# The six groups of 16 rows of each q and k stack, interleaved with a step of six rows

## The chip, the cores and the metric

The kernel runs on one core of a Trainium2 chip. The metric is the device time of one launch in microseconds (us), the median of three runs. One profiled execution gives the trace; its times are counted from the start of its span.

## What is computed

One transformer-like layer on 16 sequences: a cross-attention over a band of 129 positions, and a mixture of 16 experts with a shared expert. All is float32. The part that the change touches is the product of q and k:

```python
qkv = x @ w_in.T + b_in                      # x: layernorm of (16, 128, 512), transposed
q, k, v = jnp.split(qkv, 3, axis=-1)         # 8 heads of 16 channels, 512 positions
scores = jnp.einsum('bqhd,bkhd->bhqk', q, k) / jnp.sqrt(d)
band = jnp.abs(idx[:, None] - idx[None, :]) <= 64
attn = softmax(where(band, scores, neg))
o = einsum('bhqk,bkhd->bqhd', attn, v) ; out = w_ct(relu(o @ w_out.T) * encodings)
x = x + out ; x = x + ffn(layernorm(x))      # top-2 of 16 experts, and a shared one
```

## The kernel before, in words

Every engine has its own instruction list, written out by hand; semaphores join them. The attention part runs in steps U from -25 to 160, eight steps (`UNITS`) to a sequence, and a sequence passes through some 65 steps, so that several are under way together. In each step every engine does its share in a fixed order. The order on an engine is that of the code: an instruction that waits holds up all that stands behind it on that engine. This holds for SyncE (SP), which issues the DMAs of this part, too.

To get float32 accuracy out of bf16 matmuls, q is split into three bf16 parts (`qparts`, 128 partitions by 3 parts by 512 positions; the partition is channel times 8 plus head), and k likewise. A score is then one matmul with a contraction over 96 rows (`STACK` = 6 x 16): six pairs of parts, 16 channels each. The stacks `qstack` and `kstack` hold these rows for eight heads, [96 rows, 8 heads, 512 positions] in bf16, in a ring of four. A stack is filled by six DMAs from SBUF to SBUF. One DMA (line 305 for q, 310 for k) takes one part from all 128 partitions, 1 KB each, and writes it to 16 rows of the stack, 8 KB each: 128 KB. Group g lies in rows 16g to 16g+15. The parts become ready one after another, so the DMAs are issued in five steps: q with groups 0; 1 and 3; 2 and 4; 5 (steps -11, -10, -9, -8 of the sequence), k with groups 0; 2, 5 and 1; 4 and 3 (steps -7, -6, -5).

Line 555 (`scores`) multiplies the stacks over 96 rows, VectorE takes row maxima of the result (line 1100), GpSimd splits the maxima into three bf16 parts (lines 429 to 435), TensorE turns them, VectorE copies them to `mrows` (1108), and line 331 sends them, 24 KB, to rows 96 to 98 of `qstack` (step 9). Line 571 (`shifted_scores`, step 11) waits for this landing (`max_in`, line 567) and multiplies over 99 rows, so that the maximum is subtracted; ScalarE takes the exponential (899), GpSimd cuts the band (441, 443), and TensorE multiplies with v (585).

On SP's list, the three DMAs of line 327 (reciprocals of the sequence three before, 8 KB each, ready when GpSimd has run lines 416 to 422) stand ahead of the last q DMA (group 5 of another sequence, line 305), and this stands right ahead of line 331. Behind it come k's group 0 (310), the load of the encodings (352) and the other five DMAs of k. Line 315 fetches the denominators from every 32nd partition (`D:P:32`), so the kernel has one DMA already that steps over partitions. Before the first sequence, SP loads 6.8 MB of inputs (lines 294 to 301).

After the attention come the shared expert (385 to 520 us, with the loads of the routed experts' weights) and the routed experts, bound by TensorE.

Of the kernel before, what the change touches and what calls it, by code (L numbers as in the profile page):

```python
# [34 lines left out]
HEADS, D = 8, 16  # L35
# [11 lines left out]
STACK = 6 * D  # L47
UNITS = 2 * QB
RING = 4
# [53 lines left out]
def xattn_moe_kernel(nc, x, ctx_in, const_f, const_b, w_small, w_gu, w_d, sw_gu, sw_d, out):  # L103
    es = ExitStack()
    with es:
# [28 lines left out]
        def over(shape, dt=F32):  # L134
            cols = 1
            for s in shape:
                cols *= s
            words = cols if dt is F32 else (cols + 1) // 2
            ap = wgu[:, used[0]:used[0] + words]
            used[0] += words  # L140
            assert used[0] <= EXPERTS * 4 * 512
            if dt is not F32:
                ap = ap.bitcast(dt)
            if len(shape) == 1:
                return ap
            names = " ".join("abc"[:len(shape)])
            return ap.rearrange(f"p ({names}) -> p {names}", **{"abc"[i]: s for i, s in enumerate(shape)})

        qstack = [over([HEADS, T], BF16) for _ in range(RING)]
        kstack = [over([HEADS, T], BF16) for _ in range(RING)]  # L150
# [142 lines left out]
        def _(sp):  # L293
# [8 lines left out]

            def send_q(n, groups):
                for g in groups:
                    sp.dma_start(qstack[n % RING][D * g:D * g + D, :, :],
                                 qparts[:, Q_PARTS[g], :]).then_inc(q_in[n % RING], 16)

            def send_k(n, groups):
                for g in groups:
                    sp.dma_start(kstack[n % RING][D * g:D * g + D, :, :],  # L310
                                 kparts[:, K_PARTS[g], :]).then_inc(k_in[n % RING], 16)

            def denominators(n, g):
# [6 lines left out]
            def step(U):  # L320
# [11 lines left out]
                if (n := at(U, -11)) is not None:  # L332
                    after(sp, s2_ready, 2 * UNITS * (n - RING + 1))
                    sp.wait_ge(q_p1, n + 1)
                    send_q(n, (0,))
# [3 lines left out]
                if (n := at(U, -10)) is not None:  # L339
                    send_q(n, (1, 3))  # L340
                if (n := at(U, -9)) is not None:
                    sp.wait_ge(q_p2, n + 1)
                    send_q(n, (2, 4))
# [3 lines left out]
                if (n := at(U, -7)) is not None:  # L347
                    sp.wait_ge(k_p1, n + 1)
                    send_k(n, (0,))
# [3 lines left out]
                if (n := at(U, -6)) is not None:  # L353
                    send_k(n, (2, 5))
                    sp.wait_ge(k_p2, n + 1)
                    send_k(n, (1,))
# [1093 lines left out]
```

## Time and profile before

| | |
|---|---|
| runs | 783.01, 787.33, 787.78 us; median 787.33 us |
| profiled execution | 781.99 us, its span 780.3 us |
| TensorE busy | 670.5 us of the span (86%) |
| VectorE, ScalarE, GpSimd busy | 401.3, 355.2, 438.6 us |
| DMA, mean | 122 GB/s, 95.17 MB |
| TensorE's granted clock | 0.944 of full speed |

Busy shares are means over stages with different limits. The chain of work that ended last is read back from the last instruction, at each step to what released it. A DMA in the chain stands with the time from its issue to its landing. DMA share is the mean busy share of the core's 16 DMA engines; it can come out a little over 1.

### The profile page before, as it was taken

How to read it: one execution, taken by the hardware profiler on the slowest of the kernel's cores; microseconds unless marked ns; L12 is line 12 of the kernel's file. 1: busy time of each engine (PE TensorE's matmuls, PEld its weight loads, DVE VectorE, ACT ScalarE, POOL GpSimd, SP SyncE). 2: the span in 40 equal slices, each digit the busy share in tenths (PEclk: the TensorE clock that was granted, in tenths of full speed). 3: DMA queues.
4: the chain of work that ended last, by engine and by line, in shares of the span. 5: the costliest groups of instructions: out<-in, count | busy, mean ns of one | idle time of the engine just before them, and what ended most of it. 6: DMA issues, size and time to landing. Idle time of an engine off the chain costs nothing.

```text
span 780.3 us, 14074 instructions
## 1 busy us (share of the span) xinstructions
PE 670.5 (86%) x4136; PEld 329.9 (42%) x4136; DVE 401.3 (51%) x1439; ACT 355.2 (46%) x670; POOL 438.6 (56%) x640
## 2 busy tenths in 40 slices
PE   3179789988889988888778979989999999999992
PEld 1035445555555555553333535533333333333330
DVE  3297788888888888862332276332222322222210
ACT  2126666666666666555212111223444444444441
POOL 1377777777777777756310000023776766766763
PEclk9578999999999999998978998999999999999997
DMA  9968656666666666411496752523456465564530
GB/s 326 167 95 94 98 83 103 105 109 105 112 113 112 113 112 112 80 31 32 162 366 204 263 181 67 174 97 66 104 120 142 103 155 108 112 145 78 86 46 0
DMA packets 64472, 95.17 MB, mean 122 GB/s; under 512 B 18064, under 2 KB 42768, under 8 KB 62224
## 3 DMA queue, kind: packets, MB, share of 16 engines
q1 hardware_dynamic: 50048, 66.75, 39.3%
q0 software_dynamic: 9600, 18.89, 12.9%
q10 hardware_dynamic: 4752, 8.65, 3.4%
q8 instruction: 35, 0.57, 0.4%
q14 instruction: 37, 0.30, 0.2%
HBM read 50.99 MB, written 19.14 MB: 90 GB/s over the span
## 4 chain that ended last, share of the span: by engine, by line
PE 58%; POOL 12%; DMA 9%; issue 7%; DVE 6%; SPq 5%; ACT 3%; ACTq 0%; DVEq 0%; POOLq 0%
PE bank L731 18%; PE bank L761 9%; PE bank L718 7%; DMA wgu<-wgu 7%; PE bank L749 4%; POOL wgu L443 4%; POOL wgu L441 3%; PE bank L711 3%; SPq L327 3%; PE bank L571 3%; PE bank L555 3%; PE bank L742 2%; PE bank L585 2%; PE bank L597 2%; DVE bank L1100 2%
## 5 line engine op out<-in xcount | busy, mean ns | idle before, releaser
L1100 DVE CUSTOM_DVE_ANT_0 bank<-bank,cb 128x192 f32<-128x192 f32 (+1 forms) x512 | 187.1, 415 | 53.7 <-PE bank L555 52.4
L899 ACT ACTIVATE wgu<-bank 128x384 f32<-128x384 f32 (+1 forms) x256 | 125.2, 544 | 64.5 <-PE bank L571 64.0
L731 PE MATMUL bank<-wgu,rowsT 128*64 x320 | 147.6, 604 | 2.7 <-DVE X L1343 2.3
L733 PE MATMUL bank<-X,rowsT 128*64 128x512 f32 x320 | 147.6, 604 | 0.0
L1329 DVE TENSOR_TENSOR act_in<-act_in,bank 128x256 f32<-128x256 f32 x56 | 23.6, 421 | 214.5 <-ACT act_in L985 214.4
L555 PE MATMUL bank<-wgu 96*128 96x192 bf16 (+1 forms) x512 | 94.8, 270 | 26.0 <-DMA wgu<-wgu 15.6
L492 POOL DMA_INDIRECT rows<-xn_rows,gather_i x40 | 42.9, 1073 | 130.9 <-issue 118.8
L441 POOL TENSOR_SCALAR_AFFINE_SELECT wgu<-wgu 128x512 f32<-128x512 f32 (+1 forms) x128 | 74.5, 582 | 69.0 <-ACT wgu L899 68.6
L571 PE MATMUL bank<-wgu 99*128 99x192 bf16 (+1 forms) x512 | 73.3, 265 | 18.2 <-DMA wgu<-wgu 12.4
L508 POOL DMA_INDIRECT out<-y_out,scatter x40 | 65.6, 1639 | 38.1 <-DMA out<-y_out,scatter_i 16.4
L508 POOL DMA_INDIRECT out<-y_out,scatter_i x40 | 62.2, 1556 | 33.7 <-issue 21.6
L555 PEld LDWEIGHTS bank<-wgu 96*128 96x128 bf16 x512 | 45.5, 101 | 83.2 <-issue 56.5
L761 PE MATMUL bank<-X,actT 128*64 x160 | 75.2, 592 | 2.5 <-ACT X L1038 2.5
L443 POOL TENSOR_SCALAR_AFFINE_SELECT wgu<-wgu 128x512 f32<-128x512 f32 (+1 forms) x128 | 76.2, 595 | 0.0
L763 PE MATMUL bank<-X,actT 128*64 128x512 f32 x160 | 75.2, 592 | 0.0
L731 PEld LDWEIGHTS bank<-wgu,rowsT 128*64 128x64 f32 x320 | 40.9, 138 | 79.3 <-issue 79.3
L1100 DVE DVE_READ_ACCUMULATOR2_ANT wgu<- 128x1 f32 x512 | 71.6, 140 | 0.0
L718 PE MATMUL bank<-swgu,rowsT 128*128 128x512 f32 x128 | 67.6, 656 | 0.3 <-DVE logits L1143 0.3
L585 PE MATMUL bank<-wgu 128*32 128x192 f32 (+1 forms) x1024 | 63.9, 368 | 0.7 <-POOL wgu L443 0.7
L571 PEld LDWEIGHTS bank<-wgu 99*128 99x128 bf16 x512 | 46.2, 99 | 31.4 <-DMA wgu<-wgu 15.5
L1343 DVE COPY X<-wgu 128x2048 f32 x40 | 49.8, 1248 | 13.8 <-issue 12.6
L1038 ACT COPY X<-X 128x1024 f32 x40 | 41.8, 1045 | 27.7 <-issue 27.7
(170 smaller groups left out, 1011.5 us busy)
## 6 DMA issues: line engine op xcount, KB each, us to landing
wgu<-wgu SPq DMA_DIRECT2D x192, 128.0 KB, 4.8
wgu<-w_gu SPq DMA_DIRECT2D x16, 1024.0 KB, 7.5
X<-w_d SPq DMA_DIRECT2D x16, 512.0 KB, 3.7
out<-y_out ACTq DMA_DIRECT2D x17, 256.0 KB, 4.1
wgu<-ctx SPq DMA_DIRECT2D x16, 256.0 KB, 4.7
xn_rows<-xn SPq DMA_DIRECT2D x16, 256.0 KB, 3.1
rows<-xn_rows ACTq DMA_DIRECT2D x16, 256.0 KB, 2.8
X<-x SPq DMA_DIRECT2D x1, 3072.0 KB, 16.5
```

Of the source, the lines that this page charges most:

```text
L441: v.affine_select(out=before, in_=before, compare_op=ALU.is_ge, fill=0.0, base=off, pattern=[[0, 4], [1, P - off]], channel_multiplier=-1)
L443: v.affine_select(out=behind, in_=behind, compare_op=ALU.is_ge, fill=0.0, base=0, pattern=[[0, 4], [-1, w - P + off]], channel_multiplier= ...
L508: nc.gpsimd.indirect_dma_start(out_rows[:, :], bass.IndirectOffsetOnAxis(ap=to[0:GROUP, j:j + 1], axis=0), y_out[GROUP * g:GROUP * g + GRO ...
L555: last = mm(s1[half][:, 256 * i:256 * i + w], qstack[n % RING][0:STACK, h, P * blk:P * blk + P], kstack[n % RING][0:STACK, h, lo:lo + w], ...
L571: last = mm(s2[half][:, 256 * i:256 * i + w], kstack[n % RING][0:STACK + 3, h, P * blk:P * blk + P], qstack[n % RING][0:STACK + 3, h, lo:l ...
L585: last = mm(oacc[hg][32 * i:32 * i + 32, lo:lo + w], vaug[n % 3][:, blk, 4 * hg + i, :], probs[j % 4][:, i, 0:w], start=(blk == 0), stop=( ...
L718: last = mm(gb[k.buf][:], rowsT[:, k.buf, c, :], swgu[:, c, :], start=(c == 0), stop=(c == 3))
L731: mm(gb[k.buf][0:GROUP, :], rowsT[:, k.buf, c, 0:GROUP], wgu[:, bass.ds(e * 2048 + 512 * c, 512)], start=(c == 0), stop=(c == 3))
L733: last = mm(gb[k.buf][GROUP:P, :], rowsT[:, k.buf, c, GROUP:P], gu_half[:, k.buf, 512 * c:512 * c + 512], start=(c == 0), stop=(c == 3))
L761: mm(yb[k.buf][0:GROUP, :], actT[:, k.buf, c, 0:GROUP], wd[:, bass.ds(place * 1024 + 512 * c, 512)], start=(c == 0), stop=(c == 1))
L899: nc.scalar.activation(probs[j % 4][:, 2 * half:2 * half + 2, 0:w], s2[half][:].rearrange("p (j c) -> p j c", j=2)[:, :, 0:w], ACT.Exp, sc ...
L1100: last = v.tensor_tensor_reduce(o, o, cb[:, B_MASK + off:B_MASK + off + w], 1.0, MASKED * 2.0, ALU.add, ALU.max, rowmaxes[n % 2][:, h + i, ...
```

## The change

Group g of a stack now lies in rows g, g+6, g+12, ... g+90 in place of rows 16g to 16g+15. Both stacks are changed alike, so each row of q still meets its row of k, and the 96 rows are the same set. The number of DMAs, their order, their bytes, their sources and the runs of 1 KB that they move stay; only the rows that they write are others. Rows 96 to 98, the matmuls and all waits stay.

```diff
             def send_q(n, groups):
                 for g in groups:
-                    sp.dma_start(qstack[n % RING][D * g:D * g + D, :, :],
+                    sp.dma_start(qstack[n % RING][g:STACK:STACK // D, :, :],
                                  qparts[:, Q_PARTS[g], :]).then_inc(q_in[n % RING], 16)
 
             def send_k(n, groups):
                 for g in groups:
-                    sp.dma_start(kstack[n % RING][D * g:D * g + D, :, :],
+                    sp.dma_start(kstack[n % RING][g:STACK:STACK // D, :, :],
                                  kparts[:, K_PARTS[g], :]).then_inc(k_in[n % RING], 16)
```

## Rows read from the trace of the kernel before

**Rows 1.** The page: busy time of each engine, and slices of 19.5 us
```profile
PE 670.5 (86%) x4136; PEld 329.9 (42%) x4136; DVE 401.3 (51%) x1439; ACT 355.2 (46%) x670; POOL 438.6 (56%) x640
...
DMA  9968656666666666411496752523456465564530
GB/s 326 167 95 94 98 83 103 105 109 105 112 113 112 113 112 112 80 31 32 162 366 204 263 181 67 174 97 66 104 120 142 103 155 108 112 145 78 86 46 0
```

**Rows 2.** Windows: stretch, length, each engine's busy us, clock, DMA share, GB/s
```profile
0.00:60.00 60.00, 25.36 (x93) 12.72 (x94) 30.09 (x126) 15.54 (x25) 27.25 (x33) 0.75 0.86 194
180.00:220.00 40.00, 35.64 (x317) 21.80 (x317) 34.22 (x152) 25.88 (x52) 31.05 (x64) 1.00 0.63 107
460.00:780.00 320.00, 297.24 (x1371) 116.61 (x1369) 95.17 (x139) 125.08 (x224) 170.70 (x120) 0.97 0.45 101
```

**Rows 3.** The chain in order of time, landings in it: start, us, what
```profile
23.86 10.27 DMA wgu<-wgu
54.74 3.16 DMA wgu<-wgu
...
133.40 3.50 DMA wgu<-wgu
...
235.12 3.39 DMA wgu<-wgu
...
296.04 3.51 DMA wgu<-wgu
...
355.35 2.91 DMA wgu<-wgu
```

**Rows 4.** TensorE's timeline, 33 to 35 us: first scores, the idle time before
```profile
34.26 0.80 PE L555 MATMUL bank<-wgu 96*128 96x192 bf16 x4 [15.58 <-DMA wgu<-wgu]
```

**Rows 5.** The chain in order of time, from 232 to 241 us
```profile
232.22 0.25 POOL wgu L422
232.47 0.02 issue
232.49 0.64 SPq L327
...
234.51 0.57 SPq L305
235.07 0.04 issue
...
238.56 0.50 PE bank L571 x4
```

**Rows 6.** Waits from 133 to 342 us: total, times, longest
```profile
POOL wgu L441 <- ACT wgu L899: 41.6, 34, 2.1
PE bank L571 <- DMA wgu<-wgu: 11.1, 10, 1.2
```

**Rows 7.** Windows again, stretches in which the DMA engines are full
```profile
14.00:20.00 6.00, 3.88 (x6) 0.97 (x4) 2.29 (x4) 3.10 (x5) 2.71 (x6) 1.00 1.05 409
22.00:31.00 9.00, 0.00 (x0) 0.00 (x0) 0.03 (x1) 0.69 (x1) 3.33 (x1) 0.50 1.08 164
40.00:45.00 5.00, 3.48 (x21) 1.49 (x19) 4.89 (x25) 1.98 (x3) 3.92 (x2) 1.00 1.00 110
47.00:51.00 4.00, 3.35 (x11) 1.18 (x12) 3.88 (x22) 0.00 (x0) 1.85 (x7) 0.57 1.15 120
226.00:230.00 4.00, 4.00 (x34) 2.92 (x36) 3.01 (x16) 2.45 (x5) 3.77 (x8) 1.00 0.99 205
```

**Rows 8.** DMA issues of 44.4:44.6 and of 47.6:47.8 us: KB, us to landing
```profile
wgu<-wgu SPq DMA_DIRECT2D x1, 128.0 KB, 3.3
...
wgu<-wgu SPq DMA_DIRECT2D x1, 128.0 KB, 5.5
```

**Rows 9.** Single lines: issue ns min/median/max; landings us min/median/max, lines 305, 310
```profile
L305 SPq DMA_DIRECT2D wgu<-wgu x96: 547/602/1958, 16.7 to 315.7; - x96
...
DMA to landing us min/median/max: 3.0/4.3/10.2
...
DMA to landing us min/median/max: 3.4/5.5/10.3
...
L315 SPq DMA_DIRECT2D wgu<-wgu x32: 551/592/642, 80.4 to 377.9; - x32
```

**Rows 10.** The page: issues of all DMAs that read 128 partitions into HBM
```profile
xn_rows<-xn SPq DMA_DIRECT2D x16, 256.0 KB, 3.1
```

## The prediction

> **What bounds the kernel now.** I began with the page's busy times and slices [rows 1], then cut the run into stages with the windows [rows 2], followed the chain that ended last in order of time [rows 3, 5], and asked at each DMA in it who waits for it [rows 4, 6]. The reader is to see three things.
>
> TensorE is the bound as a whole, and alone so in the routed experts: 297 of 320 us busy behind 460 us [rows 2]. Nothing of the change reaches that stage, it can only start sooner. In the attention TensorE is busy 35.6 of 40 us, and about a tenth is idle [rows 2].
>
> Part of this idle time is a loop through the DMA queue, once per sequence. From 133.40 to 296.04 us the chain meets nine landings of the row maxima (line 331), 162.64/8 = 20.33 us apart, each 3.4 to 3.6 us long [rows 3]. Around one of them: GpSimd ends the reciprocals (L422), SP issues three small DMAs, then the last q DMA (L305, group 5), then line 331 at 235.12, which lands 3.39 us later, and only then line 571 starts at 238.56 [rows 5]. TensorE stands idle 11.1 us in ten such waits, 1.1 us each; ScalarE and then GpSimd, which closes the loop, wait for what follows [rows 6]. A landing that comes 0.1 us sooner makes the sequence 0.1 us shorter, until that 1.1 us is used up.
>
> The second place is the start. The last of the twelve DMAs for the first sequence's stacks is issued at 23.86 and lands 10.27 us later [rows 3]. TensorE is idle 15.58 us for it [rows 4], and the chain goes through it. SP had nothing to wait for there; the queue was full.
>
> **How fast the stack DMAs drain.** With the DMA engines full (share 1.0 or more), the stretches in which nearly nothing but stack DMAs run move 110 and 120 GB/s, while the loads from HBM into 128 partitions move 409 [rows 7]. So it isn't the engines' own speed: the same share of busy time moves a quarter of the bytes. Nor is it the reading side: line 338 reads 128 partitions like a stack DMA, twice the bytes, and lands in 3.1 us [rows 10]. What is left is the writing of 16 neighbouring rows. At 115 GB/s a DMA of 131 KB takes 1.14 us, and SP issues one each 0.60 us [rows 9] (0.64 with the gap), so a burst piles up: the first of six lands after 3.3 us, the last after 5.5 [rows 8]. In the steady state nobody waits for those late ones: a stack is wanted some 4 steps, 10 us, after its last DMA. Only two things are behind them in the queue and on the path: line 331, and the whole first pair of stacks.
>
> The Trainium skill (SBUF — State Buffer, Door 1: The DMA port swizzle) gives the reason a name: rows reach SBUF through 16 ports chosen by bits of the row number, and 16 neighbouring rows reach 4 of them, about 109 GB/s. The 110 and 120 GB/s agree [rows 7]. By its table rows g, g+6, ... g+90 reach 13 ports, at most two rows to a port, so at least some 218 GB/s. The sum below doesn't use this; it would be the same.
>
> **The change part by part.** *Issue:* 192 DMAs, the same number, bytes and runs. A stepped list of partitions is no dearer to issue: line 315, which steps by 32, takes 592 ns against 602 of line 305 [rows 9]. Cost 0; if it cost as much more as line 331 (0.75 against 0.60), the twelve on the path at the start and the one ahead of each of twelve line 331 would give 24 x 0.15 = 3.6 us. I take 0.
>
> *Matmuls:* the same 96 rows in another order, 0.
>
> *Rate after the change:* no row shows a stepped write of this size. From below it stays at 110 GB/s; from above it is 409, what writes to 128 partitions reach. Between them is 205 GB/s, a stretch that mixes stack DMAs with line 338's store [rows 7], and SP's issue can't feed more than 131 KB / 0.64 us = 205 GB/s. I take 205 to 409 for a standing queue, and "as fast as issued" for a burst.
>
> *The start:* at 22 us the stack DMAs and remnants of the loads stand in a full queue. From 22 to 31 us 9 x 164 GB/s = 1.48 MB moved [rows 7]; the rest went till 34.13. At 409 GB/s these 1.48 MB take 3.6 us (25.6), at 205 GB/s 7.2 us (29.2). The last issue at 23.86 plus the shortest landings of lines 305 and 310, 3.0 to 3.4 us [rows 9], sets a floor of 26.9 to 27.3. I take the middle of 27.0 and 29.5, 28.2: **gain 34.1 - 28.2 = 5.9 us**, bounds 0 (rate unchanged) and 7.2. It isn't eaten by another wait: lines 555 and the VectorE work behind it had been waiting for nothing else for 15 us [rows 4], and the second sequence's q DMAs, held by the first's landing, move ahead as well.
>
> *The loop:* line 331 lands in 3.38 to 3.58 us where the q DMA stands right ahead of it (n = 2 to 13, twelve times), and in 2.91 at 355.35, where q is no longer sent; 3.16 at the very start, where the last q DMA is 7 us old [rows 3]. Its own rows 96 to 98 don't change. What the DMA ahead leaves is 3.5 - 2.9 = 0.6 us. If that one drains twice as fast or more, I keep 0.15 for it: 3.05, a gain of 0.45 us for each landing, from 0 to 0.6 as bounds. Ten times (the nine on the chain and one of the three at its edges, where TensorE itself bounds): **gain 4.5 us**, bounds 0 and 12 x 0.6 = 7.2. TensorE's idle time there goes from 1.1 to about 0.65 us, so line 331 is still what comes last; no new wait takes over.
>
> *Off the path:* landings of lines 305 and 310 get shorter, worth nothing while stacks have 10 us of slack. SP's few long issues (up to 1958 ns [rows 9]) go.
>
> Sum: 5.9 + 4.5 = 10.4 us. The profiled execution took 781.99 us (span 780.3), so 771.6. It lies near the lowest of the runs, whose median is 787.33; against that, **787.3 - 10.4 = 776.9 us**, 1.3% faster.
>
> **The rivals.** *Only the start gains:* the 0.6 us of the loop comes from the q DMA's being there at all, its 8 rows per engine to be written and acknowledged, and not from where they go. For it: 331's packets stand behind them anyway. Against it: the first landing with q 7 us old is also 3.16, not 3.4. Time: 787.3 - 5.9 = 781.4.
>
> *No gain:* the rate of bursts is one of small SBUF-to-SBUF pieces, wherever they go. For it: all rates below 205 in rows 7 come with 1 KB pieces. Against it: 205 GB/s was reached with such pieces in the mix, and a DMA alone lands in 3.0 to 3.3 us. Time: 787.
>
> The Trainium skill (SBUF — State Buffer, The DMA setup-cost knee) says that small transfers are dominated by a fixed cost of about 2 us "and never see the port-limited rate". By it a DMA alone would gain next to nothing, as the 3.0 to 3.3 us suggest. The trace disagrees for bursts: 5.5 us for the sixth [rows 8].
>
> *Slower:* a stepped write drains more slowly than a block of rows. Place: the queue, all of the attention. In a sequence of 20.33 us twelve stack DMAs take 12 x 1.14 = 13.7 us, the rest (0.5 MB at 409 GB/s, and small ones) some 3 us; so there are 3.6 us to spare, and at over 1.44 us each (91 GB/s) the queue becomes the bound. At 1.6 us each a sequence takes 22.2 us, 1.9 us more, and with thirteen of them and the start (12 x 0.46 us) the kernel takes 787 + 30 = 817. Nothing in the rows speaks for it; only a stepped write of this size is unseen.
>
> **How the numbers follow.** Forecast 0.69, only the start 0.14, no gain 0.13, slower 0.04. The predicted time is the forecast's, 776.9. Its own range: bounds 7.2 + 7.2 give 772.9, the lower 3.5 + 2 give 781.8. Single runs lie 4.8 us apart, and the median of before is at the upper end of them, which adds some 4 us below: 769. Above, the range takes in the second rival and half of the third: 785. About 1% is what a measurement can tell from no change (779.5 to 795.2). Faster by more: 0.66, the forecast less its upper edge, plus a little of the second. Within: 0.30. Slower: 0.04.
>
> **What the profile after would show.** Bursts such as 40 to 45 us at over 180 GB/s, or at a DMA share well below 1; the share of 180 to 220 us down from 0.63 to about 0.4; the sixth DMA of a burst landing in under 4 us; the first scores (L555) near 28 us in place of 34.26; the landings in the chain at about 3.05 us and 19.9 us apart; TensorE's wait for them at 0.65 us. The issue of line 305 stays at 0.60 us. I am wrong if bursts still move 115 GB/s with a full share, or if the landings stay at 3.5, or if another engine's wait grows by what line 571's shrinks.

## The result, and the profile after

| | before | after |
|---|---|---|
| median of 22 runs each | 784.39 us | 778.97 us |
| range of the runs | 779.29 to 789.84 | 773.55 to 784.01 |
| profiled execution, span | 780.3 us | 772.4 us |
| TensorE busy, granted clock | 670.5 us, 0.944 | 672.9 us, 0.962 |

The ratio after to before is 0.993, with a 95% interval of 0.9909 to 0.9951: 0.7% faster, 5.5 us, where 10.4 us were forecast. The two profiled spans differ by 7.9 us; single executions of either kernel lie some 10 us apart, so the ratio is the measure and a pair of traces is not. Executions that took over 1.5% longer than the shortest of the same kernel are left out of the ratios below.

The page of the changed kernel: slices of 19.3 us, the SP queue's line (packets, MB, share of the 16 DMA engines' time), and the chain by engine. The queue's line and the chain's answer to those of before, where the same 66.75 MB took 39.3% and the chain had GpSimd (POOL) at 12% and VectorE (DVE) at 6%; the DMA row answers to [rows 1].

```profile
DMA  9823334433333334211577652533555555554420
GB/s 329 208 69 100 100 100 114 113 106 99 104 100 105 108 111 114 80 31 32 210 324 256 238 174 66 170 105 69 120 110 127 133 132 118 111 137 80 83 43 0
...
q1 hardware_dynamic: 50048, 66.75, 28.3%
...
PE 73%; DVE 11%; DMA 5%; issue 5%; POOL 2%; SPq 2%; ACT 1%; ACTq 0%; DVEq 0%; POOLq 0%
```

The transfers got faster: the same bytes, at 3 to 4 tenths of the DMA engines' time in the steady state where it was 6. And the chain changed its road: GpSimd's share fell from 12% to 2%, VectorE's rose from 6% to 11%. Windows of the changed kernel (start and end, length, busy us of each engine, clock, DMA share, GB/s), to be held against [rows 2, 7]:

```profile
22.00:31.00 9.00, 0.91 (x5) 0.91 (x6) 1.15 (x4) 1.30 (x2) 3.67 (x2) 1.00 0.97 202
42.60:46.40 3.80, 2.04 (x9) 0.53 (x8) 3.80 (x21) 0.62 (x1) 1.15 (x1) 1.00 0.50 138
180.00:220.00 40.00, 36.22 (x319) 21.76 (x317) 34.57 (x154) 26.18 (x52) 31.20 (x64) 1.00 0.37 102
```

The first has a full queue in its first 6 us (22 to 28 us: 222, 221 and 215 GB/s in slices of 2 us, at a share of 1.11 to 1.14) and the emptying queue behind it. The second is one burst of six stack DMAs. It leaves the DMA engines half idle: a burst is now paced by SP's issue. Its sixth DMA, issued at 45.76 us, lands as fast as the first (us to landing last; issues of 42.5:42.7 and of 45.7:45.9; the second row covers one DMA more), where before it was 3.3 and 5.5 us [rows 8]; the last fence line has the whole of line 305, [rows 9] of before:

```profile
wgu<-wgu SPq DMA_DIRECT2D x1, 128.0 KB, 2.2
...
wgu<-wgu SPq DMA_DIRECT2D x2, 128.0 KB, 2.3
...
DMA to landing us min/median/max: 2.2/2.4/8.0
```

The start, from the chain in order of time, and TensorE's timeline; before it was 10.27 us and 34.26 [rows 3, 4]:

```profile
23.02 6.93 DMA wgu<-wgu
...
30.09 0.80 PE L555 MATMUL bank<-wgu 96*128 96x192 bf16 x4 [11.27 <-DMA wgu<-wgu]
```

One sequence of the steady state: SP's two issues of line 331, then TensorE's timeline between them with the idle time before each:

```profile
228.89 0.75 SPq L331 DMA_DIRECT2D wgu<-wgu  x1
...
249.20 0.76 SPq L331 DMA_DIRECT2D wgu<-wgu  x1
...
231.70 0.50 PE L571 MATMUL bank<-wgu 99*128 99x192 bf16 x4 [0.42 <-DMA wgu<-wgu]
...
232.88 1.10 PE L597 MATMUL bank<-wgu 128*128 128x512 f32 x2 [0.45 <-DVE wgu L1120]
...
247.80 1.16 PE L612 MATMUL bank<-wgu 128*128 128x128 f32 x8 [1.02 <-DVE X L1124]
```

Line 331 is issued at 228.89 and line 571 starts at 231.70, 2.8 us later; before it was 3.44 us [rows 5]. TensorE's wait for the landing fell from 1.0 to 0.42 us. But 0.7 us later, in line 597, there is a wait of 0.45 us for VectorE's line 1120 that was not there before, and the next line 331 still comes 20.31 us after this one. The waits of ten sequences (127 to 334 us of the span: total, times, longest), [rows 6] of before:

```profile
PE bank L612 <- DVE X L1124: 10.2, 10, 1.0
...
PE bank L571 <- DMA wgu<-wgu: 5.7, 10, 0.7
...
PE bank L597 <- DVE wgu L1120: 2.7, 9, 0.5
```

So TensorE's wait for the landing lost 5.4 us in ten sequences (11.1 to 5.7), and the sequence kept its length. Half of it is there again in line 597. The rest shows as busy time for the same matmuls: 36.22 us of 40 where it was 35.64. Part of that is how the profile draws matmuls next to a wait: line 597's take 630 ns in the mean with the wait before them, 592 without.

### The profile page after: what moved, and what is told of

It is laid out like the page before. It is cut to its first block, busy times and chain, and to the rows that moved or that the text cites. A ratio compares the mean times of both kernels' runs of the same rounds, so it can differ in the third digit from the quotient of the medians.

```text
span 772.4 us, 14074 instructions
## 1 busy us (share of the span) xinstructions
PE 672.9 (87%) x4136; PEld 330.5 (43%) x4136; DVE 401.6 (52%) x1439; ACT 354.9 (46%) x670; POOL 436.2 (56%) x640
## 3 DMA queue, kind: packets, MB, share of 16 engines
q1 hardware_dynamic: 50048, 66.75, 28.3%
## 4 chain that ended last, share of the span: by engine, by line
PE 73%; DVE 11%; DMA 5%; issue 5%; POOL 2%; SPq 2%; ACT 1%; ACTq 0%; DVEq 0%; POOLq 0%
PE bank L731 18%; PE bank L761 9%; PE bank L718 6%; PE bank L585 5%; PE bank L555 5%; PE bank L571 4%; DVE bank L1100 4%; PE bank L635 4%; PE bank L749 3%; PE bank L711 3%; DMA xn_rows<-xn 3%; PE bank L612 2%; PE bank L742 2%; PE bank L606 2%; PE bank L597 2%
## 5 line engine op out<-in xcount | busy, mean ns | idle before, releaser
L508 POOL DMA_INDIRECT out<-y_out,scatter x40 | 63.4, 1584 | 36.1 <-DMA out<-y_out,scatter_i 17.4
```

Source lines behind the costliest of these rows:

```text
L508: nc.gpsimd.indirect_dma_start(out_rows[:, :], bass.IndirectOffsetOnAxis(ap=to[0:GROUP, j:j + 1], axis=0), y_out[GROUP * g:GROUP * g + GRO ...
```

## The experiments

The theory after the result, called A below: two loops of nearly one length run through each sequence. One goes through GpSimd, SP and the landing of line 331. The other is of TensorE and VectorE alone: line 612 waits for line 1124 (VectorE adds the attention's output), VectorE then works through the row maxima until line 1120 (it normalises the product with v), and line 597 waits for that. Both take 20.3 us, so shortening the first gives nothing, and the gain comes from the filling of the pipeline alone, that is, from the first scores and the sequences 1 to 3, before the distances are even. Theory B is the prediction's: one loop, through the landing.

**Only the first sequence's stacks, and all but those.** The two take the change apart.

```diff
+            def stack_rows(n, g):
+                if n == 0:            # the second kernel: n >= 1
+                    return slice(g, STACK, STACK // D)
+                return slice(D * g, D * g + D)
```

> Only the stacks of the first sequence (n = 0) are interleaved; all others lie in blocks as before. Theory A (two loops of one length): the gain of the change is made in the fill of the pipeline alone. Here the first scores start near 30 us instead of 34.3, about half of this is kept to the steady state, and the whole is 2 to 3.5 us faster (ratio 0.9955 to 0.9975); the landings of line 331 stay at 3.5 us and 20.3 us apart. Theory B (the prediction's, start 5.9 us and loop 4.5 us): 5.9 us faster, ratio 0.9925.

> All stacks but those of the first sequence are interleaved. Theory A: first scores stay near 34 us, line 331 lands in 2.9 us, but its landings in the steady state stay 20.3 us apart; 2 to 3.5 us faster, from the fill of the pipeline (sequences 1 to 3), ratio 0.9955 to 0.9975. Theory B: the loop gives 0.45 us in each of ten sequences and more of the fill, landings 19.9 us apart, 4.5 us faster, ratio 0.994.

Measured: the first alone 0.995 (0.9914 to 0.9986), 3.9 us; all the others 0.9971 (0.9943 to 0.9999), 2.3 us. Together 6.2 us, which agrees with the 5.5 us of the whole within the intervals; these are wide, 1.1 to 6.7 us and 0.1 to 4.5. The chain in order of time of the kernel with the first stacks alone (start, us, what) has the shorter start and the old landings, two of nine shown:

```profile
23.26 7.47 DMA wgu<-wgu
...
150.32 3.38 DMA wgu<-wgu
...
170.62 3.51 DMA wgu<-wgu
```

In the other kernel the chain has no landing of line 331 between 90 and 350 us, and its issues are 20.28 to 20.32 us apart. What theory B wanted from it, 19.9 us, is not there. The times alone don't decide: the first kernel's interval takes in B's 0.9925, its ratio of 0.995 lies just outside A's own 0.9955 to 0.9975, and B's 0.994 just misses the second kernel's interval. The distances decide.

**Line 331 ahead of the last q DMA, rows in blocks.** This shortens the first loop without touching the layout.

```diff
-                if (n := at(U, -8)) is not None:
+                if (n := at(U, -7)) is not None:
                     sp.wait_ge(q_p3, n + 1)
                     send_q(n, (5,))
```

> Rows in blocks as before; only SP's order is changed: line 331 is issued ahead of the last q DMA of the next sequence, not behind it. So line 331 is issued some 0.6 us sooner and has no stack DMA in front. Theory A: TensorE's wait for its landing in line 571 (1.1 us before) goes to nearly nothing, a wait for VectorE's line 1120 in line 597 takes its place, and the landings stay 20.3 us apart; total within 0.3% of before. Theory B (one loop, through the landing): landings 1.0 us closer, 19.3 us apart, 10 us faster, ratio 0.987.

Measured: 1.000 (0.9971 to 1.0029). SP's issues of line 331, and TensorE's waits from 140 to 325 us (nine sequences):

```profile
237.06 0.75 SPq L331 DMA_DIRECT2D wgu<-wgu  x1
257.37 0.76 SPq L331 DMA_DIRECT2D wgu<-wgu  x1
277.67 0.76 SPq L331 DMA_DIRECT2D wgu<-wgu  x1
...
PE bank L612 <- DVE X L1124: 9.2, 9, 1.0
PE bank L597 <- DVE wgu L1120: 7.0, 9, 0.8
```

TensorE's wait for the landing in line 571 is gone, a wait for VectorE in line 597 is there in its place, 0.8 us each, and the distance is 20.31 and 20.30. Line 331 issued one DMA sooner, with no stack DMA ahead of it, bought nothing. This is the clearest evidence against one loop.

**The kernel before once more**, for a second profile.

> The kernel before once more, for a second profile: it tells which differences between the two traces are the layout's and which come from TensorE's granted clock in the first 60 us. Theory A: first scores at 34 us, landings 20.3 us apart and 3.5 us long as in the first trace; time of the first line 331 (54.7 us before) may differ by 1 to 2 us with the clock. Theory B expects the same of this one.

Measured: one execution, 792.7 us; first scores at 33.1 us, first line 331 at 56.2, in the steady state mostly 20.3 us apart (20.39 in the mean). The stretch from first scores to first line 331 took 23.1 us in this execution and 20.5 in the first; it had TensorE's clock at 0.5 from 20 to 57 us. Over all kernels with this VectorE order it is 20.4 to 23.1 us, with either layout. The clock doesn't explain which: the first profile of the changed kernel took 23.1 us as well, at full clock throughout.

**VectorE's order, with both layouts.** If theory A holds, the second loop has to be loosened too.

```diff
             def step(U):
+                if (n := at(U, 33)) is not None:
+                    add_attention(n)                  # line 1124
                 if p := piece(U, -1):
                     maximum(*p, 0)
...
-                if (n := at(U, 33)) is not None:
-                    add_attention(n)
```

> Interleaved rows as in the changed kernel, and on VectorE the addition of the attention's output (line 1124) is moved ahead of the row maxima of its step. In the changed kernel TensorE waits 1.0 us for it in line 612, once in a sequence. Theory A (two loops of one length: one through the landing of line 331, one of TensorE and VectorE alone, through lines 1120/597 and 1124/612): with both loosened the landings of line 331 come 19.5 to 19.9 us apart (20.3 in both kernels so far), and the kernel is 4 to 8 us faster than the changed one, ratio to before 0.983 to 0.988. Theory C (something third sets 20.3 us, such as TensorE's own work): still 20.3 us apart, ratio 0.993.

> Rows in blocks as before, with the same move of line 1124 on VectorE. Theory A: the wait in line 612 goes, but the landing of line 331 (3.5 us) still holds its loop at 20.3 us, the wait in line 571 grows from 1.1 us, and the kernel gains under 0.3%: ratio 0.997 to 1.003. A theory in which VectorE's order alone had been the limit expects 19.5 us apart and a ratio of 0.988 here as well.

Measured: interleaved 0.9902 (0.9862 to 0.9941), a smaller gain than my 0.983 to 0.988 and not told from the changed kernel's 0.993; blocks 1.0039 (1.0 to 1.0078), just outside what I expected, on the slower side. The median of all twelve executions with blocks is 791.5 us against 785.0 of before, so the loss may be larger. The wait in line 612 went in both, and most of it turned up again in line 571: 11.7 us in nine sequences with interleaved rows (longest 1.5), 16.8 in nine with blocks (longest 2.0). SP's issues with interleaved rows, and windows over two sequences:

```profile
148.81 0.76 SPq L331 DMA_DIRECT2D wgu<-wgu  x1
170.12 0.76 SPq L331 DMA_DIRECT2D wgu<-wgu  x1
189.82 0.76 SPq L331 DMA_DIRECT2D wgu<-wgu  x1
...
152.00:155.40 3.40, 3.40 (x14) 1.91 (x12) 1.59 (x6) 1.56 (x3) 1.52 (x3) 0.50 0.67 199
...
170.10:189.80 19.70, 18.41 (x169) 11.16 (x165) 17.47 (x80) 13.45 (x27) 15.93 (x33) 1.00 0.40 111
```

Every second sequence is 19.7 us long, as theory A said, and every other 21.3. The long ones hold 3.4 us in which the granted clock is 0.50, which is the 1.2 GHz level; at full clock that work would take 1.7 us (an estimate, half of 3.4), and 21.3 - 1.7 = 19.6. TensorE's timeline just before:

```profile
151.79 0.67 PE L571 MATMUL bank<-wgu 99*128 99x192 bf16 x4 [1.47 <-DMA wgu<-wgu]
...
172.99 0.50 PE L571 MATMUL bank<-wgu 99*128 99x192 bf16 x4 [1.27 <-DMA wgu<-wgu]
```

The clock fell at 152.0, right behind a wait of 1.47 us; after the next one, 1.27 us, it stayed full. The length of the wait doesn't decide that: the clock also stayed full behind waits of 1.41 and 1.36 us (matmuls of 131.98 and 254.71 us), and fell behind 1.23 and 1.29 (233.43 and 274.34). In the changed kernel, where the idle time lies in three pieces of 0.42, 0.45 and 1.02 us, it doesn't fall in this stretch at all. So here the loop did get shorter, and the clock took it back.

With blocks the sequences in which the clock stays full are 20.2 us long (SP's issues of 138.38, 158.59, 178.77 and 199.05 us), those in which it falls 21.7 and 22.9 (the trace is of an execution of 793.8 us, longer than most of this kernel). So with the second loop loosened, the first holds 20.2 us by itself: the two loops of before are within 0.1 us of each other.

**All three edits together, and both orders with the rows in blocks.**

> Interleaved rows, line 1124 moved ahead on VectorE, and line 331 issued ahead of the last q DMA on SP. Theory A: the loop through the landing is 0.6 us shorter than in the kernel with the first two; if that loop bounds there, landings come 19.2 to 19.6 us apart and the kernel gains up to 5 us more (ratio 0.978 to 0.985); if the loop of TensorE and VectorE bounds there, the same time as that one. Theory C: 20.3 us apart, 0.993.

> Rows in blocks as before, with both other edits: line 1124 moved ahead on VectorE, line 331 issued ahead of the last q DMA on SP. Theory A (two loops): both loops are loosened here without the layout, so the landings of line 331 come 19.4 to 19.7 us apart, nearly as with the interleaved rows (19.45), and what the layout adds is the start alone: ratio to before 0.983 to 0.988, against 0.978 with interleaved rows. A theory in which the layout itself is needed for the shorter sequence expects 20.3 us apart and 0.997.

Measured: interleaved 0.9781 (0.9736 to 0.9826), 767.6 us where before ran 785.0 beside it; blocks 0.9931 (0.9903 to 0.996). With interleaved rows SP's issues of line 331 and a window:

```profile
203.35 0.76 SPq L331 DMA_DIRECT2D wgu<-wgu  x1
222.78 0.75 SPq L331 DMA_DIRECT2D wgu<-wgu  x1
242.23 0.76 SPq L331 DMA_DIRECT2D wgu<-wgu  x1
...
180.00:220.00 40.00, 38.22 (x330) 22.56 (x326) 35.23 (x159) 27.36 (x54) 32.72 (x68) 1.00 0.39 110
```

19.43 to 19.45 us apart, TensorE busy 38.2 of 40 us where it was 36.2, and its waits in line 571 0.7 us each. With blocks (SP's issues again):

```profile
189.89 0.76 SPq L331 DMA_DIRECT2D wgu<-wgu  x1
209.93 0.76 SPq L331 DMA_DIRECT2D wgu<-wgu  x1
229.32 0.75 SPq L331 DMA_DIRECT2D wgu<-wgu  x1
249.43 0.76 SPq L331 DMA_DIRECT2D wgu<-wgu  x1
```

Here it is 20.04, 19.39 and 20.11 us, 19.7 in the mean of the steady state, with no fall of the clock in this stretch. So my expectation was half wrong: the loops can be shortened without the layout, but not as far, and what the layout adds once both orders are changed is not the start alone but 1.5% (0.9931 to 0.9781): some 4 us of the start and 0.3 us in each of ten sequences, 3 us, explain 7 of the 12 us. The trace with blocks is of the shortest of its twelve executions (773.2 us, their median 779.1), so it can't show the rest. Why the sequences alternate with blocks, and where the rest lies, is open.

**Interleaved rows with line 331 ahead, VectorE's order as before.**

> Interleaved rows and line 331 issued ahead of the last q DMA, VectorE's order as before. Theory A: the loop through the landing is now shorter by some 1.2 us, but the one of TensorE and VectorE holds 20.3 us; TensorE's wait in line 571 goes, those in lines 597 and 612 stay (0.8 and 1.0 us); ratio to before as the interleaved rows alone, 0.991 to 0.995. Theory B (one loop): 19.1 us apart, 0.980.

Measured: 0.9929 (0.989 to 0.9967), the same as the change alone, 20.29 to 20.31 us apart. TensorE's wait in line 571 is gone, lines 597 and 612 wait 7.9 us and 9.2 us in eight and nine sequences. The first loop is shorter still, and the second holds. Theory B wanted 19.1 us and 0.980.

**Another layout: groups in pairs.** Is it the distance between the rows, or the number of row groups that one DMA reaches?

```diff
+            def stack_rows(g):
+                first = 32 * (g // 2) + g % 2
+                return slice(first, first + 31, 2)
```

> Another layout of the same stacks: groups in pairs, group 0 in rows 0, 2, ... 30, group 1 in rows 1, 3, ... 31, groups 2 and 3 in rows 32 to 63, groups 4 and 5 in rows 64 to 95. Each DMA writes over 31 rows in place of 16 (block) or 91 (interleaved). Theory P (what counts is how many of the row groups of four a DMA reaches: 8 here, 4 in a block, 16 interleaved): a stack DMA drains at up to twice the rate of a block, bursts are paced by SP's issue as in the changed kernel, landings of the sixth DMA under 3 us, line 331 in 2.9 to 3.1 us, DMA share in the steady state 0.40 to 0.45. Theory S (the rate grows with the span of rows that is written): 31 of 96 rows lie near the block, share 0.55 to 0.6, sixth landing over 4 us, line 331 in 3.3 us or more.

The window of the steady state, and the last two DMAs of a q burst (issues of 225.5:225.7):

```profile
180.00:220.00 40.00, 36.22 (x320) 21.90 (x318) 34.12 (x153) 26.00 (x51) 31.32 (x64) 1.00 0.40 110
...
wgu<-wgu SPq DMA_DIRECT2D x2, 128.0 KB, 2.9
```

The DMA share is 0.40, all but that of interleaved rows (0.37) and far from 0.63, the landing 2.9 us where it was 2.3 and 5.5; TensorE waits 0.5 us for line 331's landing, as with interleaved rows, and first scores come at 30.9 us. It is one execution, 785.5 us, so its time tells nothing; the rates are what it is for. Rows over 31 partitions do nearly what rows over 91 do. That speaks for the number of groups reached and against the span. The Trainium skill (SBUF — State Buffer, Door 1: The DMA port swizzle) has the same picture: such a DMA reaches 8 ports with two rows each, twice what 16 neighbouring rows reach. No run separates ports from other ways to count row groups, nor from the mere gap between a DMA's rows.

**The changed kernel once more.**

> The changed kernel once more, for a second profile. Theory A: landings of line 331 20.3 us apart from the fourth sequence on, in 2.8 to 3.0 us; first scores at 30 to 31 us. If the start's gain is partly eaten by TensorE's granted clock, the issue of the first line 331 lies 22 to 24 us behind the first scores where the clock is low, and 20 to 21 where it is full in most of that stretch, as in the two profiles of the kernel before (20.5 and 23.1).

Measured: one execution, 775.7 us; first scores at 29.5 us, first line 331 21.4 us later, in the steady state 20.28 to 20.32 us apart. In the steady state it agrees with the first profile. What I expected of the clock did not hold: the first profile took 23.1 us from first scores to line 331 at full clock, this one 21.4 with 3.4 us at half, and the kernel with the first stacks alone 20.4 with nearly 7 us at half.

## Why the prediction was right or wrong

| distance of line 331's issues, n = 5 to 12 | line 612's wait | us |
|---|---|---|
| before (block) | kept | 20.33 and 20.39 (two profiles) |
| block, 331 ahead | kept | 20.30 |
| interleaved (after) | kept | 20.30 (both profiles) |
| interleaved, 331 ahead | kept | 20.30 |
| block, 1124 ahead | taken away | 20.2; 21.7 and 22.9 (clock) |
| interleaved, 1124 ahead | taken away | 19.7 and 21.3 by turns (clock) |
| block, both ahead | taken away | 19.7 in the mean |
| interleaved, both ahead | taken away | 19.45 |

*The rate:* right. Stack DMAs wrote at 110 to 120 GB/s because of where the rows lay; interleaved, a full queue moves 215 to 222 GB/s (202 over the 9 us with its end), the lower end of the 205 to 409 I had taken, and a burst goes as fast as it is issued. The 13 ports of the prediction are those of groups 0 to 3; by the same table of the Trainium skill (SBUF — State Buffer, Door 1: The DMA port swizzle) groups 4 and 5 reach 14. The steady share fell from 0.63 to 0.37 (forecast 0.4).

*Issue:* right, 602 ns as before. *Matmuls:* a matmul of line 555 or 571 takes the same mean time in both kernels at full clock (246 and 273 ns, 246 and 271). The busy time as a whole, 670.5 and 672.9 us, depends on the clock as well.

*The start:* right in kind, too large in size. The step that failed is the time of the first scores, taken at 28.2 us from "the middle of 27.0 and 29.5": it is 30.1 and 29.5 in two profiles. The queue drained at some 220 GB/s, at the low end of 205 to 409 and not in the middle. Over all profiles first scores come at 32.2 to 35.7 us with blocks in the first stacks (six of them, mean 34.0), and at 29.5 to 30.9 with interleaved ones (six, mean 30.2): 3.8 us, not 5.9. TensorE's clock isn't behind it: in the first profile of before it stood at half from 20 to 38 us, in four others with blocks it was full there, with first scores from 32.2 to 35.7. The first issue of line 331 comes 4.0 us sooner in the mean of the same profiles, and the kernel with these stacks alone is 3.9 us faster (1.1 to 6.7), so nearly all of it seems to be kept.

*The landing:* underestimated. I had line 331 land at 3.05 us, it is 2.8 at the shown place; the gain is 0.6 us, the whole of my upper bound, not 0.45.

*The loop:* wrong, and this is the term that failed: "TensorE's idle time there goes from 1.1 to about 0.65 us, so line 331 is still what comes last; no new wait takes over". The wait did go to 0.57 us in the mean, and a new one in line 597 took over. 4.5 us were forecast, and in the steady state next to nothing came: 0.03 us per sequence against the first profile of before, 0.08 against the second. With this falls the sentence that a landing 0.1 us sooner makes the sequence 0.1 us shorter until the 1.1 us is used up. I had read the chain as if it were the only one of its length. The rows to see it by were in the trace: TensorE waited 1.02 us in line 612 for line 1124 in each sequence before as well, and line 597 started with no idle time, but just when VectorE's line 1120 let it. Line 1120 and line 597 in the kernel before, then line 1120 in the changed kernel, where line 597 did wait for it until 232.88:

```profile
238.33 1.28 DVE L1120 TENSOR_TENSOR wgu<-wgu,bank 128x512 f32<-128x512 f32 x2
...
239.16 1.10 PE L597 MATMUL bank<-wgu 128*128 128x512 f32 x2
...
232.05 1.28 DVE L1120 TENSOR_TENSOR wgu<-wgu,bank 128x512 f32<-128x512 f32 x2
```

It is 0.83 us from one to the other in both. In the changed kernel it is 0.83 in every sequence of the steady state, in the kernel before 0.83 to 0.99. So the slack of the second loop in the kernel before was 0 to 0.16 us, and there was next to nothing to win. (In the kernel with all three edits it is 0.83 again, so VectorE's line 1120 holds TensorE there too.)

*What took its place:* 2.3 us from the sequences 1 to 3. From the first to the fifth issue of line 331 it is 78.7 and 80.7 us in the two profiles of before, 78.6 with only the first stacks interleaved, 77.5 where only the first stacks are blocks, 74.2 and 75.3 in the two after. In this stretch the clock falls in every profile. Its mean is 0.92 and 0.91 in the two of before and 0.91 in the two kernels that take the change apart, but 0.95 in both after, which makes some 13 to 14.5 us at half clock against 7.5, about 3 us of TensorE's work (estimates, from mean and length). That is about as much as sets the changed kernel's profiles apart from 77.5. How the landings and the clock share the gain there, and whether the clock's part is the layout's doing, is open.

*The sum:* 3.9 + 2.3 = 6.2 us by the two halves, 5.5 us measured, against 5.9 + 4.5. The measured 778.97 us lies in the range and only 2.1 us above the 776.9 forecast, but that is partly luck. The sum was subtracted from 787.33 us, the median of three runs; the median of 22 is 784.39, from which the same sum gives 774.0. And about half of the 4.5 us that the loop didn't give came from a place that the sum had not named. As a ratio the result is within 1% of before, to which I gave 0.30.

## What to carry to other kernels

A chain of waits names one loop; before a gain is booked on it, look for the other waits of the same engine in that loop, and how near their releasers are to being late: the gain stops there. When two loops have one length, edits that are worth nothing alone (1.000, 1.004) brought 0.7% together, and 1.5% on top of a third. A DMA that fills 16 rows out of many is worth a try with rows that step through them: here it cost nothing to issue (602 ns both ways) and wrote at nearly twice the rate.

## What the runs showed of the hardware that was not expected

A single stack DMA, the first of its burst, also became faster: 3.3 to 2.2 us; the shortest of line 305's 96 landings went from 3.0 to 2.2. I had taken such ones to be at their floor. The Trainium skill (SBUF — State Buffer, The DMA setup-cost knee) says that small transfers never see the port-limited rate; for 128 KB written to 16 rows the trace disagrees, by 1.1 us of 3.3.

TensorE's clock fell in the steady state only in the two kernels in which its idle time was gathered into one long wait per sequence. In all others, with no wait above 1.22 us there, it stayed full. With one wait of 1.20 to 1.47 us in line 571 it fell to half for 3.4 us in every second sequence, 1.7 us of lost work. With one of 1.76 to 1.96 us it stayed full for three sequences and then fell in four of the next six, for 3.4 or 6.8 us, and that kernel was 0.4% slower than before, though no work was added. That gathering the idle time is the cause is not shown: waits of the same length stand before a fall and before none.
